# Row maxima in pairs of PSUM banks, one vector reduction for two heads

## The reference

```python
x = layernorm(x + attn(x))                 # 8 heads of 16, causal, T = 1024; scores + a rank-one term
h = x + mla_attention(rmsnorm(x))          # 16 heads of 8, causal, rotary, keys and values from a latent of 64
x = layernorm(h + moe(rmsnorm(h)))         # 4 experts of 512, each token goes to its argmax
# both attentions:
scores = where(causal, q @ k.T * scale, -inf); attn = softmax(scores, axis=-1); out = attn @ v
```

## Time and profile before

| | |
|---|---|
| time, median of 3 runs | 573.11 us (572.17 to 574.32) |
| the profiled execution, its own time | 572.96 us |
| its span, first to last instruction | 571.1 us |
| busy: PE, DVE, ACT, POOL | 492.3, 384.9, 341.3, 181.1 us |
| mean granted clock of PE | 0.946 |
| instructions L1890 (DVE, maxima) | 480, 275.8 us |
| instructions L1611 (ACT, exponentials) | 480, 240.8 us |

### The profile page before, as it was taken

One profiled execution on the slowest core, in us unless ns is written; L12 is line 12 of the kernel. 1 busy time (PEld: TensorE's weight loads), 2 busy tenths in 40 slices (PEclk: granted clock), 3 DMA queues, 4 the chain that ended last, 5 costly groups with the idle time before them and its releaser, 6 DMA issues.

```text
span 571.1 us, 10691 instructions
## 1 busy us (share of the span) xinstructions
PE 492.3 (86%) x3746; PEld 239.4 (42%) x3764; DVE 384.9 (67%) x930; ACT 341.3 (60%) x728; POOL 181.1 (32%) x249
## 2 busy tenths in 40 slices
PE   6477699988999989989969998968889987899994
PEld 3243244444443333433323343323554443357662
DVE  3287978889887877788979987887445710323343
ACT  4323167776777768767658775826466778743331
POOL 9831022237544155533111222362202205501000
PEclk9878789999999998998979998997999999999998
DMA  4994020305122002012010102031000000000010
GB/s 127 173 214 128 13 84 13 102 2 228 57 70 57 17 20 66 29 40 75 24 36 3 57 2 57 2 94 52 10 12 10 11 13 19 24 2 0 20 37 20
DMA packets 31575, 28.87 MB, mean 51 GB/s; under 512 B 8017, under 2 KB 27857, under 8 KB 31250
## 3 DMA queue, kind: packets, MB, share of 16 engines
q1 hardware_dynamic: 30626, 26.34, 16.4%
q0 software_dynamic: 896, 1.84, 1.5%
HBM read 19.27 MB, written 9.31 MB: 50 GB/s over the span
## 4 chain that ended last, share of the span: by engine, by line
PE 61%; SPq 9%; DVE 8%; ACT 8%; issue 5%; DMA 4%; POOL 2%; ACTq 1%; POOLq 0%; DVEq 0%; another core or an unknown queue 0%
PE ps L1412 16%; PE ps L1395 11%; PE ps L1376 8%; PE ps L1491 5%; DVE mparts L1890 5%; PE ps L1547 5%; ACT pr L1611 4%; SPq L1027 4%; PE ps L1477 3%; SPq L1097 2%; DMA qs<-nparts 2%; PE ps L1471 2%; PE ps L1591 2%; SPq L1019 2%; PE ps L1579 2%
## 5 line engine op out<-in xcount | busy, mean ns | idle before, releaser
L1611 ACT ACTIVATE pr<-ps 128x512 f32<-128x512 f32 (+1 forms) x480 | 240.8, 560 | 133.2 <-PE ps L1395 106.8
L1890 DVE TENSOR_REDUCE mparts<-ps 128x1 f32<-128x512 f32 (+3 forms) x480 | 275.8, 630 | 63.6 <-PE ps L1376 62.6
L1395 PE MATMUL ps<-qs,ks 64*128 64x512 bf16 (+7 forms) x558 | 136.4, 341 | 19.9 <-DMA qs<-nparts 13.4
L1376 PE MATMUL ps<-ks,qs 61*128 61x512 bf16 (+7 forms) x576 | 144.8, 349 | 7.4 <-DMA qs<-nparts 3.4
L1412 PE MATMUL ps<-pr,vs 128*32 128x512 f32 (+3 forms) x1152 | 125.6, 509 | 9.7 <-ACT pr L1611 5.1
L1217 POOL TENSOR_SCALAR_AFFINE_SELECT pr<-pr 128x512 f32<-128x512 f32 x96 | 61.2, 638 | 152.7 <-ACT pr L1611 152.2
L1395 PEld LDWEIGHTS ps<-qs,ks 64*128 64x128 bf16 (+1 forms) x576 | 42.8, 97 | 119.4 <-ACT pr L1611 46.1
L1376 PEld LDWEIGHTS ps<-ks,qs 61*128 61x128 bf16 (+1 forms) x576 | 48.8, 101 | 33.7 <-issue 11.2
L1412 PEld LDWEIGHTS ps<-pr,vs 128*32 128x32 f32 x1152 | 23.5, 108 | 47.4 <-ACT pr L1611 23.6
L1715 ACT ACTIVATE work<-ps,b 128x512 f32<-128x512 f32 x32 | 21.6, 686 | 25.0 <-PE ps L1547 24.8
L1365 PE MATMUL ps<-cmask,identb 128*128 128x128 bf16 (+1 forms) x96 | 25.1, 263 | 8.3 <-issue 7.0
(11 more groups left out here) (174 smaller groups left out, 567.3 us busy)
## 6 DMA issues: line engine op xcount, KB each, us to landing
qs<-scr0q SPq DMA_DIRECT2D x48, 64.0 KB, 2.3
qs<-scr1q SPq DMA_DIRECT2D x84, 32.0 KB
ks<-scr1k SPq DMA_DIRECT2D x84, 32.0 KB
ks<-scr0k SPq DMA_DIRECT2D x36, 64.0 KB, 2.3
scr0q<-parts SPq DMA_DIRECT2D x4, 384.0 KB, 2.8
scr0k<-parts SPq DMA_DIRECT2D x4, 384.0 KB, 3.8
scr1q<-parts SPq DMA_DIRECT2D x4, 384.0 KB, 2.5
scr1k<-parts SPq DMA_DIRECT2D x4, 384.0 KB, 3.0
```

Of the source, the lines that this page charges most:

```text
L1376: last = pe.matmul(bank[:, h, :], queries(F, 0, h0 + h, i * P, P), keys(F, 0, h0 + h, 512 * c, w), start=not diagonal, stop=True, skip_gro ...
L1395: last = pe.matmul(to[:, h, :], keys(F, 3, h0 + h, j * P, P), queries(F, 3, h0 + h, qb * 512 + lo, n), start=True, stop=True)
L1611: act.activation(pr[:, st % PSLOTS, h0:h0 + nh, 0:STEPS[st][3]], scores_at(F, v), ACT.Exp, scale=GROUPS[F][0].scale).then_inc(exped, 1)
L1890: dve.tensor_reduce(mparts[:, F % SLOTS, h0:h0 + nh, i, c], maxes_at(F, u), AX_X, ALU.max).then_inc(taken, 1)
```

## The change

A unit of maxima now covers **two banks that lie side by side**: head `h` of the lower half in the first and head `h + 2` in the second (two and two heads where the tiles are narrow). PE's matmuls alternate between the two, and one DVE instruction with twice as many columns reads both. There are 20 units in a group where there were 40, with the same columns and the same matmuls. The banks of a unit come as one of three fixed pairs, (0, 1), (2, 3) and (6, 7), at most two open; both must be free. Scores and side steps still take single banks from the same seven. `picks` goes, and the costs of a unit in `costs` are new, so that `order` makes another list.

```diff
-            out += [(i, c, (h + 2) % HG, nh, w) for h in HEADS if h % nh == 0]
+            out += [(i, c, h, nh, w) for h in range(0, HG // 2, nh)]
...
-MOST = {"scores": 3, "row maxima": 4, "side": 3}
+PAIRS = [0, 2, 6]
+MOST = {"scores": 3, "row maxima": 2, "turns": 2, "side": 3}
...
-        return [(PE, (masked + nh * w) / 2400 + 0.01 * nh), (DVE, 0.1 + nh * w / 880)]
+        rounds = 2 if GROUPS[step[1]][0].n == 0 else 1
+        return [(PE, rounds * ((masked + nh * w) / 2400 + 0.03)), (DVE, 0.15 + 2 * nh * w / 960)]
...
-        able = [b for b in banks if b not in bank_reader or bank_reader[b] in end]
-        return min(able, key=lambda b: end[bank_reader[b]] if b in bank_reader else -1.0) if able else None
+        sets = [(b, b + 1) for b in PAIRS] if user == "row maxima" else [(b,) for b in banks]
+        able = [own for own in sets if all(b not in bank_reader or bank_reader[b] in end for b in own)]
+        return min(able, key=lambda own: max(end[bank_reader[b]] if b in bank_reader else -1.0 for b in own)) if able else None
...
-            picks = [0]
-            if name[0] == "max" and last_tile is not None:
-                F = name[1]
-                left = min(len(waiting), 6)
-                same_half = [k for k in range(left) if (waiting[k][1][2] < NX0) == (waiting[0][1][2] < NX0)]
-                picks = [k for k in same_half if last_tile not in halves_of_array(waiting[k][1])][:1] or [0]
...
-            return turn_bank("max", F, u)[:, 0:nh * w].rearrange("p (h w) -> p h w", h=nh)
+            first = BANK_OF["max", F, u]
+            return ps[:, first:first + 2, 0:nh * w].rearrange("p k (h w) -> p k h w", h=nh)
...
                 for h in range(nh):
-                    last = pe.matmul(bank[:, h, :], queries(F, 0, h0 + h, i * P, P),
-                                     keys(F, 0, h0 + h, 512 * c, w),
-                                     start=not diagonal, stop=True, skip_group_check=True)
+                    for k in range(2):
+                        last = pe.matmul(bank[:, k, h, :], queries(F, 0, 2 * k + h0 + h, i * P, P),
+                                         keys(F, 0, 2 * k + h0 + h, 512 * c, w),
+                                         start=not diagonal, stop=True, skip_group_check=True)
...
-                    dve.tensor_reduce(mparts[:, F % SLOTS, h0:h0 + nh, i, c], maxes_at(F, u),
-                                      AX_X, ALU.max).then_inc(taken, 1)
+                    heads = mparts[:, F % SLOTS, :, i, c].rearrange("p (k h) -> p k h", k=2)[:, :, h0:h0 + nh]
+                    dve.tensor_reduce(heads, maxes_at(F, u), AX_X, ALU.max).then_inc(taken, 1)
```

More of the change, by code:

```diff
@@ L146 @@
 NX0 = sum(m[0] < 4 for m in MAXES)
-assert NX % 2 == 0 and NS % PSLOTS == 0
+assert NS % PSLOTS == 0
 PVB = 4
 BANKS = [0, 1, 2, 3, 5, 6, 7]
-MOST = {"scores": 3, "row maxima": 4, "side": 3}
+PAIRS = [0, 2, 6]
+MOST = {"scores": 3, "row maxima": 2, "turns": 2, "side": 3}
 def split_block(M):
@@ L344, in halves_of_array @@
 def halves_of_array(step):
[L346 to L350, removed]
+    if step[0] == "max" or GROUPS[step[1]][0].n == 0:
+        return 0, 1
+    return UNITS[step[2]][1] // 2,
 COSTS = {"rank": (PE, 0.7), "places": (DVE, 2.8), "scatter": (POOL, 1.27), "sorted": (SP, 0.4),
@@ L604, in user_of_bank @@
         return "scores"
-    if kind in ("max", "turn", "turnmax"):
+    if kind == "max":
         return "row maxima"
+    if kind in ("turn", "turnmax"):
+        return "turns"
     if kind == "proj" or kind in READER and not (kind == "expert" and step[4]):
@@ L658, in ready @@
         if user:
-            bank = choose(banks)
+            own = choose(user, banks)
             before = readers[user][-MOST[user]:]
-            if bank is None or len(before) == MOST[user] and before[0] not in end:
+            if own is None or len(before) == MOST[user] and before[0] not in end:
                 return None
-            if bank in bank_reader:
-                times.append(end[bank_reader[bank]] + HOP)
+            times += [end[bank_reader[bank]] + HOP for bank in own if bank in bank_reader]
             if len(before) == MOST[user]:
@@ L684, in kinds_left, with choose @@
         return False
-    def choose(banks):
-        able = [b for b in banks if b not in bank_reader or bank_reader[b] in end]
-        return min(able, key=lambda b: end[bank_reader[b]] if b in bank_reader else -1.0) if able else None
+    def choose(user, banks):
+        sets = [(b, b + 1) for b in PAIRS] if user == "row maxima" else [(b,) for b in banks]
+        able = [own for own in sets if all(b not in bank_reader or bank_reader[b] in end for b in own)]
+        return min(able, key=lambda own: max(end[bank_reader[b]] if b in bank_reader else -1.0 for b in own)) if able else None
     banks = [*BANKS, PVB]
@@ L696, in order @@
                 continue
-            picks = [0]
-            if name[0] == "max" and last_tile is not None:
-                F = name[1]
-                left = min(len(waiting), 6)
-                same_half = [k for k in range(left) if (waiting[k][1][2] < NX0) == (waiting[0][1][2] < NX0)]
-                picks = [k for k in same_half if last_tile not in halves_of_array(waiting[k][1])][:1] or [0]
[L703 to L706, removed]
+            at = ready(waiting[0][1], banks)
+            if at is not None:
+                best.append((at[0], waiting[0][0], name, 0, at[1]))
         _, pos, name, k, at = min(best, key=lambda x: max(x[0], 0.0) + URGENT * x[1])
@@ L715, in order @@
         if step == ("pv", 0, 0) and PVB in bank_reader:
-            freed_by[step] = bank_reader[PVB]
+            freed_by[step] = [bank_reader[PVB]]
         if user_of_bank(step):
[L718 to L721, removed]
+            own = choose(user_of_bank(step), banks)
+            bank_of[step] = own[0]
+            freed_by[step] = sorted({bank_reader[bank] for bank in own if bank in bank_reader}, key=str)
+            for bank in own:
+                bank_reader[bank] = reader_of_bank(step)
             readers[user_of_bank(step)].append(reader_of_bank(step))
@@ L1333, in wait_bank @@
             def wait_bank(*step):
-                if step in FREED_BY:
-                    reader = FREED_BY[step]
+                for reader in FREED_BY.get(step, ()):
                     if reader[0] == "scores":
```

19 lines of the change are left out of this document (11 added, 8 removed).

## The result

576.96 us (median of 4 runs, 575.48 to 583.83) against 572.92 before: ratio **1.0107** (95% interval 1.0066 to 1.0148). The forecast was 567.5 us, faster; it is 1.1% slower by the ratio, and by 4.0 us, 0.7%, by the medians. Only four runs of after stand behind both, one of them at 583.83. The profiled execution took 576.15 us, with a mean granted clock of 0.948. In all that follows, one execution of e1 and one of e4 that took over 1.5% longer than the fastest of their kernel are left out of medians, clocks and ratios.

A forecast was written before the change was run, and what follows sets the result against it. It took DVE and PE to be close to full together, holding each other up over seven shared banks. Terms -6.5 - 7.0 - 2.7 + 7.6 + 3.2 = -5.4 us took 572.96 to 567.5 us; 8-in-10 range 553 to 586.

The forecast's parts named there:

- The handovers: Turn of maxima to first exponential between groups: about 10 us in group 5 and 7 in group 6 forecast.
- Fewer scores behind a read: PE's scores steps waiting for a DVE read of maxima: 64 fewer, 12.8 us of waits, priced at -7.0 us.
- -2.7 us** of maxima: PE's maxima waiting for a read: 182 units for 270, 5.0 us less waiting, priced at -2.7 us.
- share of 0.55: Part of PE's 51.7 us of waits for DVE reads taken to be on the chain, about 28.6 us.
- merged read: DVE's reads of maxima: 240 merged pairs save 0.07 us each, 16.8 us of DVE, priced at -6.5 us.
- late start: DVE in groups 0 to 3: a read starts only when both banks are full, 0.22 us later, priced at +3.2 us.
- late release: PE's remaining waits of maxima: each read ends one bank later, 0.60 us in 23 waits, priced at +7.6 us.
- much faster: Rival: DVE sets the pace everywhere, reads give all 16.8 us and scores all 12.8, for 552 us; chance 0.08.
- Matmuls: PE: same matmuls and columns, halves of the array still filled; priced at 0, with 2.6 us either way.
- what one gains, the other loses: Handovers of groups 5 and 6 swap which has loads ahead of its maxima: 3.3 us each, counted as 0.
- two pairs are too few: Rival: DVE runs dry because PE cannot fill pairs ahead, +15.6 us, for 583 us; slower had chance 0.34.
- The clock: PE's granted clock, 0.94 to 1.00 in the stretches read; the forecast would be wrong in another way if it moved.

The follow-up runs named there:

- e1: Changed kernel with all steps behind the 36th scores unit of the last group in the order of the kernel before; 1.0055 to before, 575.8 us.
- e4: Changed kernel in its order, but two reads per unit, starting when both banks are full, each bank freed with its own read; 1.0169 to before, 580.3 us.
- e5: Changed kernel in its order, but DVE reads each bank of a pair as soon as it is full and frees it by itself; 1.0096 to before, 578.1 us.
- e10: Changed kernel's order, reading and freeing bank by bank, with any two free banks given to a pair; 1.0084 to before, 577.2 us.
- e15: Changed kernel reading bank by bank in groups 0 to 3, merged in groups 4 to 11; 1.0104 to before, 577.5 us.
- e16: Changed kernel, maxima of groups 5 and 9 ahead of loads, tail of before, bank-by-bank reads in groups 0 to 3; 1.0019 to before, 573.2 us.
- e9: Kernel before without its search for a unit of maxima in the other half of the array; 1.0098 to before, 578.2 us.
- e8: Kernel before with the maxima of groups 6 and 9 issued ahead of the blocks of loads; 0.9923 to before, 567.8 us.
- e14: Merged reads of pairs in the order of the kernel before, each pair where its later unit stood; 1.0389 to before, 594.6 us.
- e12: Kernel before with the planner's weight of wanted position against idle time changed from 0.6 to 0.5; 1.0238 to before, 585.5 us.

## Why the prediction was wrong

**Right.** The reads: 240, 1.22 us for 1.21, 260.8 us for 259; the saving is 15.0 us of DVE for 16.8. Scores' waits for DVE fell by nearly two thirds, where a third was forecast. The handovers took 10.2 and 7.3 us for 10 and 7.

**The step that failed** is the one that turned fewer waits for a read into time: "Fewer scores behind a read", **-7.0 us**, and with it the **-2.7 us** of maxima, both through the share of 0.55. e5 has the list and the banks of after, but neither the merged read nor its late start and late release, so of the sum only these two terms are left in it, -9.7 us. It came out 5.5 us slower than before (1.0096). e10, in which the banks are given out anew and 166 scores stand behind a read, not 119, is no slower for it (1.0084): how many steps have such a wait did not tell the time.

The waits as such moved as the sum had it, in part by luck. Before the share, its terms say 12.8 + 5.0 - 13.8 = 4.0 us less of waiting for reads, and 3.8 were measured (53.5 to 49.7). But scores lost 22.7 us for 12.8, and maxima gained 18.9 for 8.8. The kernel still got slower: a wait that ends in a bank being free only makes way for the next one, and scores' unnamed "issue" grew from 26.4 to 39.2 us. The share itself had no ground in a row. It sets the reads on the chain (28.6 us, out of a rounded 5%) against PE's waits for reads, and these are different things; the waits were 53.5 us, since 1.8 us in two rows of maxima were left out.

**Terms that were mis-sized.** The merged read, -6.5: about -3.7 measured. The late release, +7.6: 0.1 measured. Maxima did wait 19 us longer, but e4, which frees the first bank early, gains nothing, since its maxima wait as long. The late start, +3.2 in groups 0 to 3: e15 and e16, which undo it there, gain nothing that can be told; the 4.2 us between e4 and e5 are over all groups, and a good part goes with the clock. With the first two and these 4.2 in the sum it would have said 563.9 us (572.96 - 3.7 - 7.0 - 2.7 + 0.1 + 4.2), 13 us off. Without the -7.0 and the -2.7 it says 573.6, and of the 3.4 us that are then missing the tail is an estimate of 2.4. The "much faster" case adds up to 551 us, not 552, which changes nothing.

**What was not in the sum.** The order. The term "Matmuls", priced at 0 with 2.6 us either way, is the only one that touched it: the list without the choice of halves is 1.0% slower (e9), though that list is new in other places too. Of "what one gains, the other loses" the second half was true, yet I took a loss of 3.3 us for a constant of the kernel, and e8 shows that both handovers can be short: some 4.4 us with group 9. The tail, which the diff does not touch, had no term, though its new order could be read before any run; it cost some 2.4 us.

**The rival** "two pairs are too few" had the sign, but neither its size (583 for 577) nor clearly its mechanism. It asked for 80 us or more of DVE's wait in some 100 waits, the forecast for 62.6 or less, and 75.0 in 99 came: between the two. The place where it bites is e14, where the order was not made for it: 96.0 us in 111 waits, 594.6 us. In after, whose order was made for pairs, most of that is not there.

**The clock.** The forecast named it as what could make it wrong. Over the 29 runs of before, time goes with the mean granted clock at 3.1 us per 0.01 (correlation -0.8); in four more sets of runs of before it is 1.9 to 3.2. After has 0.945 for 0.951, an estimate of 1.9 of the 5.4 us between its median and that of the 29 runs; e9 0.938, 4.0 of 6.1; e12 0.931, 6.2 of 13.4; e5 against e4, 2.8 of 4.2. That is a correlation over runs; the pair e1 and after shows one such place. Which holes of the order make the clock fall in which run is open.

## What to carry to other kernels

Where a planner makes the order anew, hold the order in one experiment and change only the planner's weight in another before a change of a per cent is put down to the instruction that was edited: here one weight moved the same kernel by 2.4%, and the sign of the change turned with it. A wait that disappears from one row is worth nothing until the rows beside it are shown not to have grown. Small DMAs on which everything waits go ahead of a block of loads on the same queue: 0.8% here, in the kernel before. And a single trace is one draw: compare what two programs share before reading what they don't, as 5.4 of e8's 6.5 us show.

## What the runs showed of the hardware

A DVE reduction over two neighbouring PSUM banks, 1024 columns, takes 1221 ns; two reads of 512 columns on end take 1.28 us, and 683 ns is one alone. Around the hole in PE at the handover of group 9, PE's granted clock is at 0.50, the lower of its two levels (1.2 for 2.4 GHz), in before, after and e1 alike. e1 first, with the matmuls that end the hole:

```profile
392.14 0.61 PE L1442 MATMUL ps<-qs,ks 64*128 64x512 bf16 x2 [3.88 <-DMA qs<-nparts]
```

```profile
388.00:392.00 4.00, 0.26 (x2) 0.00 (x0) 2.99 (x3) 0.00 (x0) 0.00 (x0) 0.50 0.10 27
...
396.00:400.00 4.00, 3.33 (x25) 1.06 (x21) 3.15 (x3) 1.90 (x5) 1.27 (x2) 0.50 0.00 0
400.00:404.00 4.00, 4.00 (x35) 0.89 (x31) 1.33 (x2) 1.62 (x4) 0.63 (x1) 0.68 0.02 4
```

Then after:

```profile
388.61 0.61 PE L1395 MATMUL ps<-qs,ks 64*128 64x512 bf16 x2 [3.52 <-DMA qs<-nparts]
```

```profile
392.00:396.00 4.00, 2.99 (x30) 1.03 (x30) 3.73 (x4) 2.56 (x7) 1.33 (x3) 0.98 0.00 0
```

In e1 PE worked for 0.26 of the 4 us from 388, and the clock was still 0.50 when it had been busy again for 4 to 8 us; in after it was at 0.98 in the 4 us from 3.4 us behind the same matmuls. So how long it stays low differs between executions of the same instructions. A run's time goes with the clock: after's four runs are at 0.948, 0.947 and 0.948 for 575.5 to 577.8 us, and at 0.937 for 583.8.
